# An attention step in which both halves of the value products stand at the place of the second half

## The reference

```python
# first layer, self attention, in buckets of 64 (the kernel calls it ATT0)
scores = jnp.einsum('bnihd,bnjhd->bnhij', qb, kc) * scale
attn = jax.nn.softmax(jnp.where(mask, scores, -jnp.inf), axis=-1)
ob = jnp.einsum('bnhij,bnjhd->bnihd', attn, vc).reshape(B, T, C)
# cross attention with rotary position and padding (XATT0)
out = jnp.einsum('bhts,bhsd->bhtd', probs, v)
# attention inside the first mixture-of-experts block (ATT1)
ctx = jnp.einsum('bhst,bthd->bshd', attn, v).reshape(B, S, d)
# second layer, retention: decay instead of a softmax (RET)
R = jnp.einsum('bhij,bjhd->bihd', QK * D[None], V)
# cross attention in a band of 64 (XATT1)
out = jnp.einsum('bhqk,bhkd->bhqd', attn, v)
```

## Time and profile before

| | |
|---|---|
| median of three runs | 1446.69 us (1445.44 to 1448.8) |
| profiled execution, from the first to the last instruction | 1445.6 us |
| TensorE (PE) busy | 1301.3 us, 90% |
| VectorE (DVE) busy | 863.6 us, 60% |
| GpSimd (POOL) busy | 702.4 us, 49% |
| ScalarE (ACT) busy | 571.2 us, 40% |
| TensorE in the chain that ended last | 70% |
| value products (L1076), busy | 105.4 us in 2560 rows |

### The profile page before, as it was taken

One profiled execution on the slowest core, in us unless ns is written; L12 is line 12 of the kernel. 1 busy time (PEld: TensorE's weight loads), 2 busy tenths in 40 slices (PEclk: granted clock), 3 DMA queues, 4 the chain that ended last, 5 costly groups with the idle time before them and its releaser, 6 DMA issues.

```text
span 1445.6 us, 33878 instructions
## 1 busy us (share of the span) xinstructions
PE 1301.3 (90%) x12165; PEld 1048.3 (73%) x12165; DVE 863.6 (60%) x2071; ACT 571.2 (40%) x1272; POOL 702.4 (49%) x949
## 2 busy tenths in 40 slices
PE   5998889989999999989999999959998999929887
PEld 4666647976777777767899899846766777628776
DVE  3788853337888888736622111258885778773346
ACT  1555545433444555643222222214443455414331
POOL 4566642017777466630233333237785555427426
PEclk9999989998999999979999999979999999959999
DMA  6000000020000000000389998631000000038954
GB/s 255 2 2 0 1 1 30 1 86 17 14 15 5 2 17 15 16 16 1 131 317 325 334 332 316 233 139 31 0 17 9 24 30 22 17 105 303 312 176 145
DMA packets 47371, 137.79 MB, mean 95 GB/s; under 512 B 6926, under 2 KB 29647, under 8 KB 41105
## 3 DMA queue, kind: packets, MB, share of 16 engines
q1 hardware_dynamic: 32944, 110.37, 21.7%
q0 software_dynamic: 7536, 19.67, 4.4%
q10 hardware_dynamic: 6768, 6.16, 1.2%
HBM read 119.54 MB, written 17.56 MB: 95 GB/s over the span
## 4 chain that ended last, share of the span: by engine, by line
PE 70%; DVE 12%; DMA 8%; issue 5%; POOL 3%; ACT 2%; DVEq 0%; SPq 0%; POOLq 0%; ACTq 0%
PE ps L1114 11%; PE ps L981 9%; PE ps L1032 9%; PE ps L1349 8%; PE ps L1076 6%; PE ps L1056 4%; PE ps L1047 4%; PE ps L1361 4%; DMA row_in<-rows_of,from_u 4%; DMA back_of<-w_odd 3%; PE ps L925 2%; PE ps L972 2%; DVE negmax L1791 2%; PE ps L1083 2%; PE ps L1007 2%
## 5 line engine op out<-in xcount | busy, mean ns | idle before, releaser
L1415 ACT ACTIVATE probsT_all<-ps 128x1024 f32<-128x1024 f32 x128 | 131.1, 1025 | 164.0 <-PE ps L981 164.0
L1791 DVE TENSOR_REDUCE negmax<-ps 128x8 f32<-128x1024 f32 x128 | 156.0, 1219 | 59.4 <-PE ps L981 59.2
L1349 PE MATMUL ps<-hT,w_tile 128*128 128x128 f32 x1304 | 161.9, 278 | 0.6 <-ACT act_sb L1673 0.2
L1349 PEld LDWEIGHTS ps<-hT,w_tile 128*128 128x128 f32 x1304 | 153.3, 193 | 3.1 <-issue 0.8
L981 PE MATMUL ps<-qe,kf 32*128 32x256 f32 x1280 | 153.1, 387 | 0.0
L981 PE MATMUL ps<-ke,qf 32*128 32x256 f32 x1024 | 146.0, 403 | 0.0
L759 POOL TENSOR_SCALAR eps_sum<-mv 128x1 f32<-128x1 f32 x112 | 25.5, 228 | 199.1 <-DVE mv L1728 112.2
L981 PEld LDWEIGHTS ps<-qe,kf 32*128 32x128 f32 x1280 | 111.0, 188 | 4.8 <-issue 2.8
L1076 PE MATMUL ps<-probsT_all,va 128*32 128x128 f32 x2560 | 105.4, 283 | 7.6 <-ACT probsT_all L1415 4.4
L2354 DVE TENSOR_TENSOR h_in<-ps,act_sb 128x512 f32<-128x512 f32 x39 | 27.0, 692 | 140.0 <-PE ps L1349 140.0
L700 POOL DMA_INDIRECT back_of<-be,to_u x39 | 39.4, 1010 | 140.4 <-DVE be L2367 140.4
(11 more groups left out here) (288 smaller groups left out, 3350.9 us busy)
## 6 DMA issues: line engine op xcount, KB each, us to landing
w_tile<-in_w_f SPq DMA_DIRECT2D x29, 1536.0 KB, 7.5
w_tile<-in_w_f SPq DMA_DIRECT2D x47, 385.0 KB, 7.0
y_back<-in_w_f SPq DMA_DIRECT2D x10, 1536.0 KB
back_of<-w_odd ACTq DMA_DIRECT2D x47, 128.0 KB, 6.5
ctxT<-in_ctxT SPq DMA_DIRECT2D x32, 128.0 KB, 2.1
rows_of<-nv SPq DMA_DIRECT2D x32, 128.0 KB, 1.7
w_even<-in_w_att SPq DMA_DIRECT2D x3, 1024.0 KB, 7.2
y_back<-back_of SPq DMA_DIRECT2D x6, 512.0 KB, 5.7
```

What stands on the lines that cost most here:

```text
L1349: last = mm(ps[:, 2 * which + at.two, fc * P:(fc + 1) * P], w[:, col:col + P], rowT[:, at.two, c, :], start=c == 0, stop=c == KC - 1)
L1415: nc.scalar.activation(half_of(probsT_all, half), ps[:, 2:4].rearrange("p b n -> p (b n)"), ACT.Exp, scale=HD ** -0.5).then_inc(S["probs"], 1)
L1791: nc.vector.tensor_reduce(m, ps[:, 0:2].rearrange("p b (h k) -> p (b h) k", h=HB), AX.X, ALU.max, negate=True).then_inc(S["s_max"], 1)
```

## The change

In the four softmax layers `weigh_values(now, 0)` moves from its place behind `project_values` to the place just ahead of `weigh_values(now, 1)`, so past `first_units`, `turn_normed`, the scores of half 1, `turn_in`, `out_project` and `logits`. In RET it moves past `turn_in` (and in the last RET step past a half of XATT1's scores). Nothing else is changed; the other engines' lists are the same.

```diff
@@ -1168,11 +1168,11 @@
                         project_values(at[1])
                     if late:
                         out_project(late, at)
-                    weigh_values(now, 0)
                     if 3 in at:
                         turn_in(at[3], at)
                     if to_max:
                         scores(by_query(to_max, 0))
+                    weigh_values(now, 0)
                     weigh_values(now, 1)
                     if to_max:
                         scores(by_query(to_max, 1))
@@ -1184,8 +1184,6 @@
                     turn_out(done, at)
                 if 1 in at:
                     project_values(at[1])
-                if now:
-                    weigh_values(now, 0)
                 first_units(normed(at))
                 turn_normed(normed(at), at)
                 scores((by_query(to_max, 1) if to_max else []) + (by_key(now, 1) if now else []))
```

## The result

The changed kernel takes 1422.79 us (median of 4 runs, 1418.68 to 1427.61), the kernel before 1446.07 in the same series (4 runs, 1443.99 to 1448.80). The ratio is 0.9856, with a 95% interval of 0.9821 to 0.989: faster by 1.4%, some 21 to 23 us, where 4.5 were forecast and 1438.2 was the lower end of the range. The sign was right, the size was not.

A forecast was written before the change was run, and what follows sets the result against it. It took a VectorE-TensorE ring to bound ATT0 and TensorE itself XATT0, ATT1 and XATT1. Terms -4.0 + 1.4 + 1.2 + 0.7 + 0.0 - 3.8 = -4.5 us gave 1442.2 us from 1446.7, range 1438.2 to 1447.5.

The forecast's parts named there:

- ATT0, 11 steps: In ATT0 the scores of half 1 start 0.36 us earlier, period 10.98 in place of 11.34: 4.0 us gained.
- XATT0, 14 steps: In XATT0 TensorE newly idles for red0; cost 0.10 us a step, between 0 and 0.21: 1.4 us lost.
- ATT1, 12 steps and the first ones: In ATT1 0.06 us net lost in 12 steps, 0.7, plus 0.5 for the first steps: 1.2 us lost.
- XATT1, 14 steps: In XATT1 0.53 us gained against 0.58 for the moved work: 0.05 a step, 0.7 us lost.
- RET: In RET TensorE runs the moved instructions without waits in either order, so nothing changes: 0.0 us.
- Fill and drain: At seven places where pipelines fill or drain, 0.55 us gained each: 3.8 us, between 1.0 and 5.0.
- the ring: ATT0's bound: red1, VectorE's list with `inj`, red0, scores of half 1, red1 again; 11.34 us becomes 10.98.
- The wait for `inj`: TensorE's wait in each ATT0 step, claimed to fall from 0.64 us to about 0.5.
- (a): Scores' weight load exposed behind new waits in 54 softmax-layer steps: 10.3 us on top, +5.8, 1452.5 us; chance 0.12.
- The price of 107 ns: Estimate from the skill's weight-load rule, per step behind a wait: 5.8 us in 54 steps, sum +1.3, 1448.0 us.
- (b): ScalarE or GpSimd binds ATT0 as tightly, or saturated layers pay in full: -0.5, 1446.2 us; chance 0.24.
- (c): Earlier red1 and `inj` give back all loss in XATT0, ATT1 and XATT1: -7.8, 1438.9 us; chance 0.10.

## Why the prediction was wrong

Its terms against what the profiles show, in us:

| Term of the sum | forecast | shown |
|---|---|---|
| ATT0, 11 steps | -4.0 | -2.3 (11 x -0.21) |
| XATT0, 14 steps | +1.4 | +0.3 (14 x 0.02) |
| ATT1, 12 steps and the first ones | +1.2 | -0.2 (12 x -0.05, and +0.4 in the first two) |
| XATT1, 14 steps | +0.7 | -1.5 (14 x -0.11) |
| RET | 0.0 | -2.6 (11 x -0.30 and +0.7 late) |
| Fill and drain | -3.8 | -14.4 |
| Sum | -4.5 | -20.7 |

Of the 23.7 us between the spans, 3 lie outside the terms: 1.4 in RET's first step (8.66 and 7.24 us in the two profiles of the kernel before), 1.2 in MOE0 behind its first part, the rest around the MLP. The cause of these stays open. By size the miss is 10.6 us in fill and drain and 7.3 in the four middle terms, with 1.7 the other way in ATT0.

**The step that failed first**, in the order of the sum, is the one in which WV0 was given one price: "eight instructions, that take 150.78 - 150.21 = 0.57 us", moved as they are. From it follow RET's 0.0 and the losses of the three saturated layers. The runs showed that a group has a price of its own, 0.13 us, and lengthens its neighbours by about as much again: one group more in RET +0.28, joining in RET -0.3, in the softmax layers -0.15 to -0.26. It could have been read from the trace of before, had I looked inside the group: inside WV0 four rows start every 0.11 us, which makes 0.44 for 16 and not the 0.57 that they take. I compared WV0 only with itself.

**The second**, and the larger, is the size of "7 x 0.55 = 3.8 us" for fill and drain. The rows on which it rested said "TensorE at its lower clock level by these rows", and I took the low clock as given and priced the work at it. That the level itself could change was not in the sum. At the end of ATT1 2.8 + 3.2 + 0.9 = 7.0 us are gained behind the last tile's first exp, shown by the kernel that changes three tiles alone. At least 4.8 of them are the clock's, and 1.0 is that of the group that left the place; part is chance, as one profile in five of the early groups fell for 3.4 us only. Of the rest, the steps there gave 2.2 us, the end of ATT0 3.5 (two steps of 10.29 and 10.50 became 9.51 each, and the last exp comes 1.7 earlier), its first two steps 0.7, the end of XATT1 1.0. At the end of ATT0 the clock is in it too: it was low for 20.5 and 23.9 us in the two profiles of the kernel before and for 13.6 in both of the changed one, and those two steps together took from 20.6 to 24.7 us over the profiles with the groups as before there. How much of the 3.5 us is the clock's isn't shown. The reading beside it was a little off as well: 1.08 us is the row's length, the group takes 1.01 from start to start, against 0.57 at the full clock, so less than twice. (And the attention layers cover some 830 us, not 600; that is what the five windows cover.)

**What held.** In ATT0 the ring was the right one: SC1 starts 0.06 us after red0 in place of some 0.4, and the gain is all of the place and none of the joining. Its size was off by 0.15 us a step, because the list of VectorE was taken as a constant 9.20, while 0.90 of it was standing still beside GpSimd, and 1.05 is now. The wait for `inj` stayed at 0.63 rather than falling to 0.5. The first steps of ATT1 cost 0.4, where 0.5 were in the sum. The new idle for red0 stands where it was foretold: 0.30 and 0.23 ahead of L948 in the two steps of XATT0 looked at, 0.36 ahead of L972 in ATT1, and the wait ahead of L1032 is gone; XATT1 has 0.13; the place alone costs 0.17, 0.21 and 0.04 a step there, where 0.10, 0.06 and 0.05 were in the sum and 0.21, 0.22 and 0.10 were its bounds. One of them:

```profile
403.38 0.39 PE L948 MATMUL ps<-pad_bf,ones_bf 32*128 32x512 bf16 x2 [0.30 <-DVE negmax L1790]
```

**The rivals.** (a), the weight load that lies open behind the new wait, did not come: SC1's first matmul runs 0.06 us after red0's end in every step of the four layers in which it waits for it, but for two of ATT1 with 0.13, and 0.15 had been the mark for it. The first load does lie behind the wait: it starts at 132.34, 0.05 after red0's end, and the matmul 0.01 after it, at 132.35. So the load's length isn't exposed behind these waits. The price of 107 ns that was worked out beside it is not borne out in any layer. (b), another ring in ATT0, was wrong for ATT0, and true for RET, where nobody had put it: the ring of GpSimd and VectorE is 0.3 us below TensorE's. (c) came nearest: the saturated layers did not pay, but not because an earlier red1 gave the time back. It was the joining, as the late but separate groups show: without it they pay. All cases together reached to 1438.2; none of them held a gain in TensorE's own work or in the clock.

## What to carry to other kernels

A group of small-tile matmuls among full-array work isn't worth its rows alone: price it at rows and a fixed part, and look for the fixed part by comparing groups of different length and the same neighbour in and out of their company, before saying that a move "costs what the moved work costs". Where rows of a drain show the low clock, ask whether the change lifts it, and price the whole low stretch as a case of its own. And when TensorE gets room, or an operation of VectorE is shifted against GpSimd, read the other engines' rounds first: here the next ring in RET, through GpSimd and VectorE, lay 0.3 us below, and the best version came from making GpSimd start later by one wait, while one wait later still lost it again.

## What the runs showed of the hardware that was not expected

- Value products (128x32 tiles, 128 columns) take 0.35, 0.57 and 1.01 us in groups of 8, 16 and 32 rows between other matmuls: 0.13 us a group beside 0.0275 a row. The full-array work beside them takes more too: two transposes 0.06 us between two groups (0.37 and 0.31), and 0.15 when a group stands between them, the output projection 0.09 (1.03 and 0.94).
- A VectorE operation on 16 numbers in a partition takes 0.17 us, and 0.57 to 0.73 where a GpSimd add over 256 runs when it starts; it ends 0.03 to 0.04 us behind that add. This held for tensor_scalar, for tensor_tensor with two SBUF inputs, and for both data types. A tensor_scalar on 256 numbers took 1.12 in place of 0.41 beside a longer GpSimd product.
- Behind a wait of TensorE for a reduction the first weight load starts 0.05 us after the reduction's end and the matmul 0.01 after that (ATT0).
- TensorE's granted clock fell to 1.2 GHz for 17.1 us (once 3.4) at the end of ATT1 in each profile with the groups there as before, and in none with the joined late groups in its last three tiles. With late but separate groups it fell for 3.4 us. TensorE's busy time in the windows of 5 us just ahead of it and around it, 82 to 84% in the kernel before and 77 to 91% in the two kernels where it didn't fall, doesn't tell them apart.
